# Causal attention with a full-array product ahead of each plain score, one DMA for each set of fixed rows, and another order of GpSimd's first steps

## The chip, the cores and the metric

The program runs on one NeuronCore of a Trainium2 chip. The metric is device time in microseconds (us), the median of three executions. Besides these one execution was taken with the hardware profiler; all rows of a trace shown here come from it.

## What is computed

A decoder of four layers on x of shape (8, 256, 128). Each layer adds an attention block and then a feed-forward block to x, each on a layer norm of x. The context has shape (8, 512, 128), and there are 16 heads of 8 dimensions. Layer 2 has a causal attention inside its feed-forward block, and this is the stage that the change touches most:

```python
def attention(x, wq, wk, wv, wo, bo):
    b, t, _ = x.shape
    q = (x @ wq).reshape(b, t, HEADS, HEAD_DIM)
    k = (x @ wk).reshape(b, t, HEADS, HEAD_DIM)
    v = (x @ wv).reshape(b, t, HEADS, HEAD_DIM)
    scores = jnp.einsum('bqhd,bkhd->bhqk', q, k)
    mask = jnp.arange(t)[:, None] < jnp.arange(t)[None, :]
    scores = jnp.where(mask, -jnp.inf, scores)
    attn = jax.nn.softmax(scores / np.sqrt(HEAD_DIM), axis=-1)
    ctx = jnp.einsum('bhqk,bkhd->bqhd', attn, v).reshape(b, t, EMB)
    return ctx @ wo + bo
```

The other attentions (layers 0 to 3, called A0 to A3) go over the 512 positions of the context, A2 with a mask.

## The kernel before

The stages run in the order A0, F0, A1, F1, A2, AS, F2, A3, F3 (PHASES): A are attentions, F feed-forward blocks, AS is the causal attention with 256 keys. Every engine has its own program, written out by hand, and they meet at semaphores. An attention stage has one body per batch (8), a body four groups `g` of four heads, and a group four steps `k`. A body on TensorE (`body` in `attention`) issues at each step, in this order: two plain scores, then transposed scores, then products of probabilities and values, and in fixed places one product of the projections (`misc`: XT, Q, K, V, turns of the head sums AVT0 and AVT1, ONT, O).

Plain scores (`scores`, L1032 to L1043) serve only to find the largest score of each row. Q and K of a head lie on a strip of 32 partitions, four heads on the four strips, each with its eight dimensions in several parts and some fixed rows. A plain score is one product, 32 rows high, of 128 queries with the keys; in AS only with the keys that the queries see, so 128 columns for the first half of the queries and 256 for the second. VectorE takes the maximum (`maximum`), in AS after adding `caus_q`. The scores run two groups ahead: those of a batch's groups 0 and 1 are issued in the body before, and the first two groups of AS in the last body of A2. GpSimd splits the maxima, TensorE turns them into rows of Q, and the transposed scores (`scores_T`) come out with the maximum already subtracted. In AS steps 0 and 3 of a group each hold two units of transposed scores: a product of 256 columns, one of 128, and the mask, which is a full-array product of the identity `ident_b` with `caus_T` (L1062). ScalarE takes the exponential, and `values` multiplies by V (L1086).

The parts of Q and K go through DRAM: SyncE (SP) saves them as rows of a scratch tensor and loads them back as strips (`save_k`, `save_q`, `load_strips`). A strip has 32 rows. Rows 1 to 24 are the parts; row 0 and rows 25 to 31 are fixed (ones where the maxima and the keys' mask enter, zeros otherwise). They are made once: GpSimd lays a pattern into `fixed`, TensorE spreads it with a product with ones, VectorE copies it to `rows_q` and `rows_k`, and SP fills both buffers of the scratch (`fill_rows`), two DMAs for Q and two for K each time. Between the two fills SP issues the loads of F0's weights, of the rest of x and of the next context.

At the start GpSimd computes the power of -1/2 for the first quarter of x (`first_power(0)`), clears the value tile of batch 0 (`set_values(0)`), computes the other three powers, and only then normalises batch 0 (`normalise_batch`), which TensorE, ScalarE and GpSimd need for Q. VectorE takes the statistics of all of x, waits for the four powers and then quantises the weights of F0 (`quantise_weights`) before it takes the first maximum.

Of the kernel before, what the change touches and what calls it, by code (L numbers as in the profile page):

```python
# [36 lines left out]
B, S, D, SK = 8, 256, 128, 512  # L37
H, DH = 16, 8
NT = B * S // 128
QT = S // 128  # L40
HG = 4
STRIP = 32
K_ROWS = (1, 1 + 2 * DH, 1 + DH)
Q_ROWS = (1, 1 + DH, 1 + 2 * DH)
MAX_ROW = 1 + 3 * DH
MASK_ROWS = (0, MAX_ROW + 3)
NG = H // HG
TB = 4
NBLK = NT // TB
# [116 lines left out]
def build(nc, t, out):  # L166
    cnt = Counts()
    with ExitStack() as ctx:
# [6 lines left out]
        sig = {n: sem(n) for n in cnt.names}  # L175
# [52 lines left out]
        fixed = sb("fixed", [1, 2, 128])  # L228
# [180 lines left out]
        def _(sp):  # L409
# [11 lines left out]

            def fill_rows(p):

                for n, fill, w in (("q", rows_q, S), ("k", rows_k, SK)):
                    rest = scratch[n][p].rearrange("(h r) w -> r h w", h=H)
                    for r0, r1 in ((0, 1), (MAX_ROW, STRIP)):
                        sp.dma_start(rest[r0:r1], fill[r0:r1, :].rearrange("r (o w) -> r o w", o=1).to_broadcast([r1 - r0, H, w]))\
                          .then_inc(strips_filled[p], 16)

            def load_rest():  # L430

# [126 lines left out]
            for ph in PHASES:  # L558
                if ph not in ATT:
                    continue  # L560
                if ph != "AS":

                    if ph != "A0":
                        wait(sp, "v_ready", cnt.start("v_ready", ph))
                        first_contexts(ph)
                    if ph in ("A1", "A2"):

                        wait(sp, "o_ready", cnt.start("o_ready", ph))
                        a = {"A1": "A2", "A2": "AS"}[ph]
                        for i, w in enumerate("qkvo"):  # L570
                            sp.dma_start(w_att[a][:, i, :], t[f"{a}_{w}"]).then_inc(watt_in[a], 16)
                    if ph == "A0":
                        for p in range(2):
                            sp.wait_ge(strips_filled[p], 16 * 4)
                    if ph == "A3":
                        wait(sp, "max_done", cnt.start("max_done", ph))
                        save_mask(Batch(0))
                    wait(sp, "st_ready", cnt.start("st_ready", ph))
                    save_k(ph, Batch(0))
                    save_q(ph, Batch(0))  # L580
                    load_strips(ph, Batch(0))
                    next_context(ph, Batch(2))
                    if ph == "A3":
                        save_mask(Batch(1))
                    save_k(ph, Batch(1))
                    save_q(ph, Batch(1))
                    load_strips(ph, Batch(1))

                def body(bt, first, last):
                    nph, nbt = following(ph, bt, 2)  # L590
                    cph, cbt = following(ph, bt, 3)
                    if nph:
                        if nph == "A3":
                            save_mask(nbt)
                        if nph != "AS":
                            save_k(nph, nbt)
                        if cph and cph != "AS":
                            next_context(cph, cbt)
                        save_q(nph, nbt)
                        if nph == "AS":  # L600
                            save_k(nph, nbt)
                        wait(sp, "st_ready", cnt.at("st_ready", ph, bt, cnt.per[ph]["st_ready"] - 1))
                        load_strips(nph, nbt)
                    if ph in ("A1", "AS", "A3") and bt.b < 4:
                        load_ffn({"A1": "F1", "AS": "F2", "A3": "F3"}[ph], bt.b)

                batches(body)
                if ph == "A0":
                    load_rest()
# [8 lines left out]
        def _(pool):  # L618
# [3 lines left out]
            link(pool.memset(fixed[:, :, :], 0.0))  # L622
            link(pool.memset(ones_row[:, :], 1.0))
            for r in MASK_ROWS:
                pool.memset(fixed[:, 0, r:r + STRIP * (HG - 1) + 1:STRIP], 1.0)
            link(pool.memset(fixed[:, 1, :].rearrange("p (j r) -> p j r", j=HG)[:, :, MAX_ROW:MAX_ROW + 3], 1.0))
            pool.memset(w_att["A3"][:, 0:3, :], 0.0).then_inc(rows_made, 1)
            link(pool.memset(ident[:, :], 0.0))
            link(pool.affine_select(out=ident[:, :], in_=ident[:, :], compare_op=ALU.not_equal, fill=1.0, base=0, pattern=[[-1, 128]], channel_multiplier=1))
# [96 lines left out]
            def attention(ph):  # L726
                b0, b1 = Batch(0), Batch(1)
                if ph != "AS":
# [2 lines left out]
                    normalise_batch(ph, b0)  # L731
                    split_k(ph, b0)
                    split_q(ph, b0)
                    normalise_batch(ph, b1)
                    if ph == "A0":
                        set_values(1)
                    if ph == "A3":
                        prepare_masks(b1)
# [82 lines left out]
                pool.memset(vaug[p][:, :, :, DH:DH + 1], 1.0).then_inc(vaug_set, 1)  # L821

            first_power(0)
            set_values(0)
            for blk in range(1, NBLK):
                first_power(blk)
            for ph in PHASES:
                if ph in ATT:
                    attention(ph)
# [193 lines left out]
        def _(pe):  # L1023
# [8 lines left out]
            def scores(ph, bt, g, i):  # L1032
# [5 lines left out]
                if ph == "AS":  # L1038
                    nk = 128 * (q + 1)
                wait(pe, "max_done", cnt.at("max_done", ph, bt, 8 * g + i) - BACK[i])  # L1040
                dst = ps_s[TURN[i]][:, 0:nk]
                pe.matmul(dst, qst[p][strip, g, q * 128:(q + 1) * 128], kst[p][strip, g, 0:nk],  # L1042
                          start=True, stop=True).then_inc(sig["s_ready"], 1)  # L1043

            def scores_T(ph, bt, g, n, c):

# [761 lines left out]
```

## Time and profile before

| | us |
|---|---|
| median of three executions (2041.43 to 2043.42) | 2042.76 |
| the profiled execution | 2041.18 |
| its span, first to last instruction | 2039.4 |
| TensorE busy | 1857.1 (91%) |
| VectorE busy | 1151.3 (56%) |
| ScalarE busy | 1096.2 (54%) |
| GpSimd busy | 590.7 (29%) |
| mean granted clock of TensorE | 0.896 |

The page names the engines PE (TensorE), PEld (its weight loads), DVE (VectorE), ACT (ScalarE), POOL (GpSimd) and SPq (SP's queue). PEclk is the clock that was granted to TensorE as a share of 2.4 GHz, in tenths in the 40 slices of the span (9 is 0.9 or more). A row of the timeline has its start, its length, engine, line, operation, what it writes and reads, the rows and columns of the array that it uses, and its shape; "x4" are four instructions merged. A matmul's length contains its way through the array, so matmuls overlap, and the distance of starts tells what each one costs.

### The profile page before, as it was taken

Reading aid. Unit: us, or ns where it says so; the run is one execution under the profiler, and the core shown is the slowest. Engines: PE = TensorE matmul, PEld = TensorE weight load, DVE = VectorE, ACT = ScalarE, POOL = GpSimd, SP = SyncE. Lnnn points to the kernel's source line nnn. Section 1 sums busy time; section 2 is a strip of 40 time slices with the busy share of each in tenths; the row PEclk is TensorE's granted clock in tenths of the full one; section 3 lists DMA queues with packets and bytes.
Section 4 is the critical chain, followed back from the end, with each engine's and each line's share of the span. In section 5 each row is a group of like instructions: output and inputs, shape, how many; then the busy total and the mean of one; then the engine's idle time right before and its main releaser. Section 6 shows DMA issues by size and latency. Waiting matters only on the chain.

```text
span 2039.4 us, 38938 instructions
## 1 busy us (share of the span) xinstructions
PE 1857.1 (91%) x14476; PEld 1195.3 (59%) x14476; DVE 1151.3 (56%) x3394; ACT 1096.2 (54%) x2172; POOL 590.7 (29%) x1171
## 2 busy tenths in 40 slices
PE   3999965899979999899999999997997999989997
PEld 1455534455559988634444555556885455569997
DVE  4788845688842233267777533334664788834342
ACT  0788840588854444256666533333331788854443
POOL 4344312233221222123333422212333444212221
PEclk9999987799989999889999855557997899989999
DMA  4433200445300000132322322100002454100000
GB/s 121 130 120 120 72 16 25 130 150 170 97 7 1 1 1 1 59 114 81 115 69 68 99 82 64 55 25 1 1 1 69 140 160 148 57 1 6 6 6 6
DMA packets 114882, 132.38 MB, mean 65 GB/s; under 512 B 14962, under 2 KB 78728, under 8 KB 114696
## 3 DMA queue, kind: packets, MB, share of 16 engines
q1 hardware_dynamic: 114696, 129.90, 21.1%
q8 instruction: 117, 1.92, 0.4%
q14 instruction: 69, 0.57, 0.1%
HBM read 83.45 MB, written 46.40 MB: 64 GB/s over the span
## 4 chain that ended last, share of the span: by engine, by line
PE 77%; DVE 8%; issue 7%; ACT 4%; POOL 1%; DMA 1%; SPq 0%; POOLq 0%; DVEq 0%
PE ps_av L1086 13%; PE ps_s L1311 13%; PE ps_s L1042 13%; PE ps_t L1289 9%; PE ps_t L1058 5%; DVE mx L1443 4%; PE ps_s L1289 3%; PE ps_t L1071 3%; PE ps_m L1142 2%; PE ps_m L1094 2%; PE ps_m L1128 2%; ACT prob L851 2%; PE ps_m L1134 2%; PE ps_t L1062 2%; PE ps_m L1121 2%
## 5 line engine op out<-in xcount | busy, mean ns | idle before, releaser
L851 ACT ACTIVATE prob<-ps_t 128x512 f32<-128x512 f32 (+1 forms) x1152 | 628.9, 583 | 229.5 <-PE ps_t L1058 145.6
L1443 DVE TENSOR_REDUCE mx<-ps_s 128x1 f32<-128x512 f32 x768 | 491.2, 683 | 117.5 <-PE ps_s L1042 110.3
L1042 PE MATMUL ps_s<-kst,qst 32*128 32x512 f32 (+2 forms) x1280 | 380.8, 514 | 42.2 <-DVE mx L1443 26.7
L1086 PE MATMUL ps_av<-prob,vaug 128*32 128x256 f32 (+1 forms) x4608 | 379.3, 405 | 3.2 <-ACT avs L892 3.2
L1058 PE MATMUL ps_t<-qmx,kst 32*128 32x256 f32 (+1 forms) x2304 | 339.4, 347 | 0.1
L1042 PEld LDWEIGHTS ps_s<-kst,qst 32*128 32x128 f32 x1280 | 159.3, 204 | 274.6 <-issue 151.1
L1311 PEld LDWEIGHTS ps_s<-w_ffn,prob 128*128 128x128 f32 x2688 | 314.1, 192 | 8.3
L1311 PE MATMUL ps_s<-w_ffn,prob 128*128 128x128 f32 x2688 | 318.4, 275 | 0.0
L991 ACT ACTIVATE prob<-ps_t,b1c 128x512 f32<-128x512 f32 x204 | 125.3, 685 | 240.1 <-PE ps_t L1289 240.1
L1677 DVE SCALAR_TENSOR_TENSOR avs<-ps_s,comb,avs 128x128 f32<-128x128 f32 x336 | 94.6, 344 | 260.4 <-PE ps_s L1311 260.4
L788 POOL TENSOR_TENSOR kst<-w_ffn,kst 128x512 fp32r<-128x512 f32 x100 | 127.1, 1273 | 370.5 <-ACT kst L976 370.5
L1058 PEld LDWEIGHTS ps_t<-qmx,kst 32*128 32x128 f32 x2304 | 211.6, 197 | 21.5 <-issue 19.1
L1446 DVE CUSTOM_DVE_ANT_0 junk<-ps_s,mask_q 128x512 bf16<-128x512 f32 x256 | 167.7, 687 | 72.2 <-PE ps_s L1042 72.2
L692 POOL CAST mpart<-mx 128x8 bf16<-128x8 f32 x160 | 34.8, 218 | 587.4 <-DVE mx L1443 317.4
L1289 PE MATMUL ps_t<-k_hi,kst 128*128 128x512 f32 x600 | 184.7, 415 | 6.2 <-ACT xfT L953 2.4
L1086 PEld LDWEIGHTS ps_av<-prob,vaug 128*32 128x32 f32 x4608 | 94.6, 111 | 112.9 <-issue 44.4
L1446 DVE CUSTOM_DVE_ANT_0 junk<-ps_s,caus_q 128x128 bf16<-128x128 f32 (+1 forms) x256 | 82.6, 354 | 127.8 <-PE ps_s L1042 126.5
L1289 PEld LDWEIGHTS ps_t<-k_hi,kst 128*128 128x128 f32 x600 | 107.7, 193 | 28.1 <-DVE prob L1662 3.6
L647 POOL TENSOR_TENSOR rstd<-veps,neg_half 128x2 f32<-128x2 f32 (+1 forms) x60 | 48.4, 807 | 259.5 <-DVE means L1387 259.5
L896 ACT ACTIVATE qmx<-ps_m 128x256 fp32r<-128x256 f32 x160 | 61.8, 387 | 97.8 <-PE ps_m L1096 97.7
L1071 PE MATMUL ps_t<-mask_T,ident_b 128*128 128x512 bf16 x256 | 82.1, 388 | 5.3 <-ACT prob L851 3.6
L1289 PE MATMUL ps_t<-k_lo,kst 128*128 128x512 f32 x300 | 85.4, 393 | 0.0
(209 smaller groups left out, 2202.1 us busy)
## 6 DMA issues: line engine op xcount, KB each, us to landing
kst<-k_parts SPq DMA_DIRECT2D x128, 256.0 KB, 3.5
qst<-q_parts SPq DMA_DIRECT2D x160, 128.0 KB, 3.8
k_parts<-k_hi SPq DMA_DIRECT2D x64, 256.0 KB, 3.0
q_parts<-q_hi SPq DMA_DIRECT2D x80, 128.0 KB, 2.4
ctxT<-in_ctxT SPq DMA_DIRECT2D x32, 256.0 KB, 2.7
k_parts<-k_lo SPq DMA_DIRECT2D x32, 256.0 KB, 3.2
q_parts<-q_lo SPq DMA_DIRECT2D x40, 128.0 KB, 2.4
w_ffn<-in_F_w SPq DMA_DIRECT2D x18, 256.0 KB, 6.6
```

The source lines that it names most:

```text
L788: pool.tensor_tensor(halves(wl), first_weights(ph, e), halves(wh.bitcast(F32)), ALU.subtract).then_inc(sig["wl_done"], 1)
L851: nc.scalar.activation(row[:, S * kt:S * kt + w], ps_t[TURN[unit(ph, g, n) % 8]][:, 0:w], ACT.Exp).then_inc(sig["exp_done"], 1)
L991: nc.scalar.activation(h[:, c, :], src, ACT.Gelu, bias=b1c[:, 4 * e + c:4 * e + c + 1]).then_inc(sig["h_done"], 1)
L1042: pe.matmul(dst, qst[p][strip, g, q * 128:(q + 1) * 128], kst[p][strip, g, 0:nk], start=True, stop=True).then_inc(sig["s_ready"], 1)
L1058: mm = pe.matmul(dst, kst[p][strip, g, kt * 128:(kt + 1) * 128], qmx[strip, g % 2, seen(ph, kt):], start=mask in (None, "keys") or mask == ...
L1071: pe.matmul(ps_t[TURN[turn]][:, :].rearrange("p (c s) -> p c s", c=2), ident_b[:, :], mask_T[:, 2 * kp:2 * kp + 2, :], start=True, stop=False)
L1086: mm = pe.matmul(ps_av[32 * j:32 * j + 32, q0:S], vaug[p][:, kt, HG * g + j, :], prob[:, buf, j, S * kt:S * (kt + 1) - q0], start=(kt == 0 ...
L1289: mm = pe.matmul(ps_h[c][:, :], w[:, 128 * c:128 * (c + 1)], x[:, :], start=(n == 0), stop=(n == 2))
L1311: mm = pe.matmul(dst, h[:, c, 128 * q:128 * (q + 1)], w2c, start=(c == 0 and not bias), stop=(c == nc_h - 1))
L1443: dve.tensor_reduce(mx[:, buf, i:i + 1], src, AX.X, ALU.max, negate=True).then_inc(sig["max_done"], 1)
L1446: dve.tensor_tensor_reduce(junk[:, TURN[i], 0:nk], src, m, -1.0, 3.0e38, ALU.add, ALU.min, mx[:, buf, i:i + 1])\
L1677: ins = dve.scalar_tensor_tensor(out=acc[:, q, :], in0=src, scalar=comb[:, q, n:n + 1], in1=acc[:, q, :], op0=ALU.mult, op1=ALU.add)
```

## The change

In `scores`, each plain score of AS gets a product ahead of it into the same bank: `ident_b` times the columns 128 to 255 of the first block of `caus_T`, which are all zeros, over all 128 rows; the score then adds to it (`start=False`). That makes 256 products more, half of them of 128 columns and half of 256. The fixed rows move to the front of each strip (rows 0 to 7), so one DMA fills them for Q and one for K, from 128 partitions of `rows_q` and `rows_k` in place of eight. On GpSimd `set_values(0)` moves behind the split of batch 0's Q, and the other three first powers behind batch 1's normalisation.

```diff
@@ -40,9 +40,10 @@
 QT = S // 128
 HG = 4
 STRIP = 32
-K_ROWS = (1, 1 + 2 * DH, 1 + DH)
-Q_ROWS = (1, 1 + DH, 1 + 2 * DH)
-MAX_ROW = 1 + 3 * DH
+FIXED = 8
+K_ROWS = (FIXED, FIXED + 2 * DH, FIXED + DH)
+Q_ROWS = (FIXED, FIXED + DH, FIXED + 2 * DH)
+MAX_ROW = 1
 MASK_ROWS = (0, MAX_ROW + 3)
 NG = H // HG
 TB = 4
@@ -421,11 +422,8 @@
 
             def fill_rows(p):
 
-                for n, fill, w in (("q", rows_q, S), ("k", rows_k, SK)):
-                    rest = scratch[n][p].rearrange("(h r) w -> r h w", h=H)
-                    for r0, r1 in ((0, 1), (MAX_ROW, STRIP)):
-                        sp.dma_start(rest[r0:r1], fill[r0:r1, :].rearrange("r (o w) -> r o w", o=1).to_broadcast([r1 - r0, H, w]))\
-                          .then_inc(strips_filled[p], 16)
+                for n, fill in (("q", rows_q), ("k", rows_k)):
+                    sp.dma_start(scratch[n][p].rearrange("(h r) w -> h r w", h=H)[:, 0:FIXED, :], fill).then_inc(strips_filled[p], 16)
 
             def load_rest():
 
@@ -571,7 +569,7 @@
                             sp.dma_start(w_att[a][:, i, :], t[f"{a}_{w}"]).then_inc(watt_in[a], 16)
                     if ph == "A0":
                         for p in range(2):
-                            sp.wait_ge(strips_filled[p], 16 * 4)
+                            sp.wait_ge(strips_filled[p], 16 * 2)
                     if ph == "A3":
                         wait(sp, "max_done", cnt.start("max_done", ph))
                         save_mask(Batch(0))
@@ -622,8 +620,8 @@
             link(pool.memset(fixed[:, :, :], 0.0))
             link(pool.memset(ones_row[:, :], 1.0))
             for r in MASK_ROWS:
-                pool.memset(fixed[:, 0, r:r + STRIP * (HG - 1) + 1:STRIP], 1.0)
-            link(pool.memset(fixed[:, 1, :].rearrange("p (j r) -> p j r", j=HG)[:, :, MAX_ROW:MAX_ROW + 3], 1.0))
+                pool.memset(fixed[:, 0, r:r + FIXED * (H - 1) + 1:FIXED], 1.0)
+            link(pool.memset(fixed[:, 1, :].rearrange("p (h r) -> p h r", h=H)[:, :, MAX_ROW:MAX_ROW + 3], 1.0))
             pool.memset(w_att["A3"][:, 0:3, :], 0.0).then_inc(rows_made, 1)
             link(pool.memset(ident[:, :], 0.0))
             link(pool.affine_select(out=ident[:, :], in_=ident[:, :], compare_op=ALU.not_equal, fill=1.0, base=0, pattern=[[-1, 128]], channel_multiplier=1))
@@ -731,8 +729,12 @@
                     normalise_batch(ph, b0)
                     split_k(ph, b0)
                     split_q(ph, b0)
+                    if ph == "A0":
+                        set_values(0)
                     normalise_batch(ph, b1)
                     if ph == "A0":
+                        for blk in range(1, NBLK):
+                            first_power(blk)
                         set_values(1)
                     if ph == "A3":
                         prepare_masks(b1)
@@ -821,9 +823,6 @@
                 pool.memset(vaug[p][:, :, :, DH:DH + 1], 1.0).then_inc(vaug_set, 1)
 
             first_power(0)
-            set_values(0)
-            for blk in range(1, NBLK):
-                first_power(blk)
             for ph in PHASES:
                 if ph in ATT:
                     attention(ph)
@@ -1039,8 +1038,11 @@
                     nk = 128 * (q + 1)
                 wait(pe, "max_done", cnt.at("max_done", ph, bt, 8 * g + i) - BACK[i])
                 dst = ps_s[TURN[i]][:, 0:nk]
+                if ph == "AS":
+                    pe.matmul(dst.rearrange("p (c s) -> p c s", s=128), ident_b[:, :], caus_T[:, 0:1, 128:S].to_broadcast([128, q + 1, 128]),
+                              start=True, stop=False)
                 pe.matmul(dst, qst[p][strip, g, q * 128:(q + 1) * 128], kst[p][strip, g, 0:nk],
-                          start=True, stop=True).then_inc(sig["s_ready"], 1)
+                          start=ph != "AS", stop=True).then_inc(sig["s_ready"], 1)
 
             def scores_T(ph, bt, g, n, c):
```

TensorE, a stretch of a body of AS behind the first products with V of a group: two steps without transposed scores, the turn of the maxima between them (`L1094`, `L1096`; after the change `L1096`, `L1098`). Before:

```order
L1042 MATMUL ps_s<-kst,qst 128x128 x2
L1094 MATMUL ps_m<-qst,ident_r 128x256
L1096 MATMUL ps_m<-ident_b,mpart 128x128 x2
L1042 MATMUL ps_s<-kst,qst 128x256 x2
L1121 MATMUL ps_m<-xnT,w_A 128x256
L1086 MATMUL ps_av<-prob,vaug 32x128 x4
```

After, the same place:

```order
L1042 MATMUL ps_s<-caus_T,ident_b 128x128
L1044 MATMUL ps_s<-kst,qst 128x128
L1042 MATMUL ps_s<-caus_T,ident_b 128x128
L1044 MATMUL ps_s<-kst,qst 128x128
L1096 MATMUL ps_m<-qst,ident_r 128x256
L1098 MATMUL ps_m<-ident_b,mpart 128x128 x2
L1042 MATMUL ps_s<-caus_T,ident_b 128x256
L1044 MATMUL ps_s<-kst,qst 128x256
L1042 MATMUL ps_s<-caus_T,ident_b 128x256
L1044 MATMUL ps_s<-kst,qst 128x256
L1123 MATMUL ps_m<-xnT,w_A 128x256
L1088 MATMUL ps_av<-prob,vaug 32x128 x4
```

Each plain score now stands behind a product of 128 rows. Of the two pairs the first follows products with V, the second a product of 128 rows and 128 columns (`L1098`), as before.

TensorE at a step that also has transposed scores (`L1060`), after the change, behind the product of K (`L1130`):

```order
L1130 MATMUL ps_m<-xnT,w_A 128x256
L1042 MATMUL ps_s<-caus_T,ident_b 128x128
L1044 MATMUL ps_s<-kst,qst 128x128
L1042 MATMUL ps_s<-caus_T,ident_b 128x128
L1044 MATMUL ps_s<-kst,qst 128x128
L1060 MATMUL ps_t<-qmx,kst 128x256 x2
L1060 MATMUL ps_t<-qmx,kst 128x128
L1064 MATMUL ps_t<-caus_T,ident_b 128x2x128
L1060 MATMUL ps_t<-qmx,kst 128x128
```

The pair follows a full product here too; the transposed scores follow the second score.

GpSimd at the start, from the first power on. Before:

```order
L815 TENSOR_TENSOR rstd<-veps,neg_half 128x4
L820 MEMSET vaug 128x2048
L821 MEMSET vaug 128x64
L815 TENSOR_TENSOR rstd<-veps,neg_half 128x4 x3
L707 TENSOR_SCALAR xn<-x_tok,means,rstd 128x128 x2
L673 CAST k_hi<-kf 128x512
L675 TENSOR_TENSOR k_lo<-kf,k_hi 128x512
L681 CAST q_hi<-qf 128x256
L683 TENSOR_TENSOR q_lo<-qf,q_hi 128x256
L707 TENSOR_SCALAR xn<-x_tok,means,rstd 128x128 x2
L820 MEMSET vaug 128x2048
```

After:

```order
L817 TENSOR_TENSOR rstd<-veps,neg_half 128x4
L705 TENSOR_SCALAR xn<-x_tok,means,rstd 128x128 x2
L671 CAST k_hi<-kf 128x512
L673 TENSOR_TENSOR k_lo<-kf,k_hi 128x512
L679 CAST q_hi<-qf 128x256
L681 TENSOR_TENSOR q_lo<-qf,q_hi 128x256
L822 MEMSET vaug 128x2048
L823 MEMSET vaug 128x64
L705 TENSOR_SCALAR xn<-x_tok,means,rstd 128x128 x2
L817 TENSOR_TENSOR rstd<-veps,neg_half 128x4 x3
L822 MEMSET vaug 128x2048
```

The power's rows (`L815`, now `L817`) for the other three quarters move from ahead of batch 0's normalisation to behind batch 1's.

## Rows read from the trace of the kernel before

**Rows 1.** The page: busy time of each engine, and the granted clock in 40 slices.

```profile
PE 1857.1 (91%) x14476; PEld 1195.3 (59%) x14476; DVE 1151.3 (56%) x3394; ACT 1096.2 (54%) x2172; POOL 590.7 (29%) x1171
...
PEclk9999987799989999889999855557997899989999
```

**Rows 2.** Busy time by stretches: A2, then four of AS.

```profile
core 0: us, PE busy (x) PEld busy (x) DVE busy (x) ACT busy (x) POOL busy (x), PEclk, DMA share, GB/s
1000.00:1034.00 34.00, 33.42 (x313) 15.06 (x314) 24.85 (x88) 23.29 (x49) 13.06 (x29) 1.00 0.30 90
1143.00:1160.00 17.00, 16.30 (x143) 9.66 (x139) 9.68 (x64) 9.89 (x24) 9.08 (x23) 1.00 0.20 54
1160.00:1183.00 23.00, 22.93 (x122) 13.00 (x120) 8.93 (x53) 8.40 (x19) 6.03 (x18) 0.50 0.35 106
1183.00:1353.00 170.00, 168.18 (x907) 92.25 (x910) 62.29 (x379) 63.62 (x146) 40.55 (x117) 0.50 0.23 67
1353.00:1389.00 36.00, 31.11 (x173) 16.95 (x169) 8.77 (x45) 10.94 (x26) 3.10 (x10) 0.50 0.00 0
```

**Rows 3.** Timeline of TensorE, AS: start, length, line, tiles, shape; turns and K's products.

```profile
1140.72 0.60 PE L1142 MATMUL ps_m<-ident,avs 128*128 128x128 f32 x4
...
1152.24 0.60 PE L1128 MATMUL ps_m<-xnT,w_A 128*128 128x256 f32 x2
...
1216.03 1.06 PE L1128 MATMUL ps_m<-xnT,w_A 128*128 128x256 f32 x2
...
1231.61 1.06 PE L1142 MATMUL ps_m<-ident,avs 128*128 128x128 f32 x4
...
1250.05 1.06 PE L1128 MATMUL ps_m<-xnT,w_A 128*128 128x256 f32 x2
```

**Rows 4.** Timeline of TensorE, AS at granted clock 0.50.

```profile
1223.04 0.39 PE L1062 MATMUL ps_t<-caus_T,ident_b 128*128 128x256 bf16 x1
1223.36 0.47 PE L1058 MATMUL ps_t<-qmx,kst 32*128 32x128 f32 x1
1223.77 0.39 PE L1062 MATMUL ps_t<-caus_T,ident_b 128*128 128x256 bf16 x1
...
1226.78 0.47 PE L1042 MATMUL ps_s<-kst,qst 32*128 32x128 f32 x2
1227.18 0.58 PE L1094 MATMUL ps_m<-qst,ident_r 128*128 128x256 f32 x1
...
1227.93 0.58 PE L1042 MATMUL ps_s<-kst,qst 32*128 32x256 f32 x2
1228.44 0.66 PE L1086 MATMUL ps_av<-prob,vaug 128*32 128x128 f32 x8
```

**Rows 5.** Timeline of TensorE, AS at granted clock 1.00.

```profile
1147.58 0.28 PE L1062 MATMUL ps_t<-caus_T,ident_b 128*128 128x256 bf16 x1
1147.79 0.32 PE L1058 MATMUL ps_t<-qmx,kst 32*128 32x128 f32 x1
1148.05 0.28 PE L1062 MATMUL ps_t<-caus_T,ident_b 128*128 128x256 bf16 x1
```

**Rows 6.** Timeline of all engines, the first 45 us.

```profile
8.39 1.04 POOL L815 TENSOR_TENSOR rstd<-veps,neg_half 128x4 f32<-128x4 f32 x1
...
18.86 2.57 SPq L427 DMA_DIRECT2D k_parts<-prob  x2
...
25.57 1.01 POOL L815 TENSOR_TENSOR rstd<-veps,neg_half 128x4 f32<-128x4 f32 x1 [0.45 <-DVE means L1387]
...
28.81 1.21 SPq L496 DMA_DIRECT2D k_parts<-k_hi  x2
...
36.55 0.69 DVE L1472 TENSOR_REDUCE aw<-ps_av 128x4 f32<-128x512 f32 x1 [11.06 <-PE ps_av L1176]
...
38.30 0.80 PE L1042 MATMUL ps_s<-kst,qst 32*128 32x512 f32 x3 [1.89 <-DMA qst<-q_parts]
...
43.81 1.28 DVE L1443 TENSOR_REDUCE mx<-ps_s 128x1 f32<-128x512 f32 x2
```

## Prediction

> **What bounds the kernel now.** I read the page first: TensorE is busy for 91% of the span, and the row of granted clocks shows one long stretch of fives, slices 23 to 27, in a kernel that otherwise runs near full clock [rows 1]. Then the busy time by stretches [rows 2]. In A2, the masked attention, TensorE is busy for 33.4 of 34 us at clock 1.00. In the causal stage AS it is as busy (168.2 of 170 us), and the clock stands at 0.50 (1.2 of 2.4 GHz). It fell at about 1160, in the second batch's body of AS, after a stretch that was 96% busy, and did not come back before the stage's end. ScalarE, VectorE and GpSimd are busy for 64, 62 and 41 of those 170 us, so TensorE alone sets the pace of AS, and what an added product costs there is what it takes on TensorE.
>
> How long a body (one batch) takes at either level: from K's product to K's product is 34.0 us at 0.50; the stretch from the second turn of the head sums to K's product is 18.44 us at 0.50 and 11.52 at 1.00 [rows 3]. The ratio 0.625 makes a body 21.3 us at full clock, 12.7 less. That is the prize the full-array product could win; what matters is what it costs and whether it wins it.
>
> Now a pair of scores goes strip, strip, and its two products start together (x2 on one row, 0.40 us to the next product). With the change it goes full, strip, full, strip. Added are two full streams, one strip stream that ran beside the other, two exchanges to strip and one to full: at half clock 3 x 0.107 + 2 x 0.11 + 0.30 = 0.84 us for a pair of 128 columns and 3 x 0.213 + 0.52 = 1.16 for one of 256; at full clock 0.16 + 0.40 = 0.56 and 0.32 + 0.40 = 0.72. Where a full product stands ahead of the pair (two of a group's four pairs: those of steps 0 and 2), the exchange it pays today goes: minus 0.11. A group has two pairs of each width: 2 x 0.84 + 2 x 1.16 - 0.22 = 3.8 us at half clock, 2 x 0.56 + 2 x 0.72 - 0.22 = 2.35 at full. A batch (four groups): 15.1 and 9.4 us. Both ends of this price: if every exchange hid behind a running product, only 16 x 128 + 16 x 256 = 6144 columns would be left, 5.1 us a batch at half clock, 2.6 at full; nothing makes it cheaper, since TensorE has no idle time there. The upper end is 16.0 at half clock, every pair paying its whole exchange. I take 15.1: the measured exchanges are between the same two shapes with the same identity as weights.
>
> The Trainium skill says the same in "TensorE: Matmul & The Clock Gate", Part 3: small products run side by side when they lie in different row groups, and a weight load overlaps a running product only if its row group differs; a full-array load shares a row group with everything. The trace agrees (strip pairs start together, the mask product does not).
>
> **Does the clock hold?** At full clock the body would grow from 21.3 to 30.7 us; of the 9.4 added, 2.6 stream columns through the whole array and 6.8 are exchanges or strips that no longer run side by side. In A2, which keeps 1.00, a step adds two masks of 512 columns, nearly all streaming [rows 2]. So AS gains work for the array but spreads its own over 44% more time, and it fell before after 1.25 bodies at full clock. I forecast that it falls again, about in the middle of the first body, and stays down: at half clock the body is 34.0 + 15.1 = 49 us, and of the 15.1 only 5.1 stream columns through the whole array, so the stage grows longer faster than it grows denser.
>
> **Sum for AS.** The scores run two groups ahead, so the 32 groups lie thus: two in A2's last batch and two in AS's first body at full clock, 4 x 2.35 = 9.4 us; 28 at half clock, 28 x 3.8 = 106. The clock falls 0.75 body earlier in the work: 0.75 x 12.7 = 9.5. Together +125 us. Everything else of AS stays (F2 starts at half clock today too), and VectorE, ScalarE and the DMAs have more time, so they hide as before.
>
> **The start.** GpSimd today waits with batch 0's normalisation until the last power at 25.57, which needs all of x; K, Q and V of batch 0, and behind them VectorE's weight quantisation, begin late (36.55), and the first maximum comes at 43.81 [rows 6]. With the change xn follows the first power, which ends at 9.4. From the last power's end, 26.6, to the quantisation takes 10.0 us today, so what lies between is done near 20. VectorE still needs all four powers: 26.6, or some 2.4 us sooner, since one DMA for each fill takes SP about 0.6 (as each k_hi save: 1.21 for two) and not 1.3 (2.57 for two), and the x load lies behind one set of four. The quantisation takes 43.81 - 36.55 = 7.3: VectorE is free at 31.5 to 33.9. The scores need batch 0's strips: from first save to first score is 9.5 us today (28.81 to 38.30), some 8.5 when q waits with k; the save waits for the second fill. Its issue ends at 21.4 today, 16.7 then; landing 3 us later gives scores at 28; landing as late as today gives 37. So the first maximum comes at 31.5 to 37.5: 6 to 12 us won. I take 11, since 128 partitions are read in place of eight. No later step waits for a fixed time, so it stays. GpSimd's clearing of the value tile (two memsets, about 2 us) now stands ahead of ScalarE's V copy; the maximum's start covers it.
>
> **Total.** 2041.2 (profiled execution) + 125 - 11 = 2155; the median of the runs is 1.6 higher and I round to **2155 us**.
>
> **The rivals.**
> A, *the clock holds* although the exchanges cost what I say. For it: the products are of the full array, A2 and F2 hold 1.00 with such. Against: AS fell in a 96% busy stretch. Seven bodies of 30.7 make 215 in place of 222 (from 1131, a body of 21.3 before K's last product at full clock, to 1353), A2's end +4.7, the last 36 us [rows 2] at 0.625 plus two groups 27.2 (-8.8): -11, start -11: **2019**. It decides if the granted clock is 1.00 through AS.
> B, *the exchanges hide and the clock holds*: bodies 21.3 + 2.6 = 23.9, seven 167 (-55), last stretch -12, A2's end +1.3, start -11: **1964**. Against it: the exchange rows above.
> The Trainium skill speaks for B in the same page, Part 2: weights for the background buffer may be loaded ahead of products in flight, and Part 1 has the clock follow a busy engine. By these the change would win; the first is not what the mask product's rows show, and by the second AS should not have fallen at 96% busy.
> C, *the exchanges hide but the clock falls*: 28 x 1.28 + 4 x 0.64 + 9.5 - 11 = +37: **2078**.
> D, *the clock falls late*: each body that stays at full clock saves 49.1 - 30.7 = 18.4; three more make **2100**.
> E, *start alone counts*, the two effects in AS cancelling: near 2041.
>
> **Chances.** Forecast 0.68, D 0.08, C 0.06: slower by over 0.2% 0.82 (0.2%, 4 us, is about what a measurement of this kernel can tell from none). A 0.08, B 0.07: faster 0.15. E 0.03. The forecast's own range is 2125 to 2178 (price per group 3.4 to 4.0, fall anywhere from A2's end to the second body, start 6 to 12). The range takes in C and D: 2072 to 2178, and leaves out A, B and E.
>
> **What would show it.** Right: the clock row at fives from the first batch of AS on, K's product to K's product 49 us, full-strip-full starts 0.3 to 0.4 apart, an AS busy near 100%; the first maximum near 33. Wrong: tens through AS (A or B; the body's length, 31 or 24, tells which), or a body of 39 us at half clock (C).

## The result, and the profile after

The changed kernel takes 2152.46 us (median of three, 2150.2 to 2155.99) against 2042.76: ratio 1.054, 95% interval 1.0516 to 1.0565. Its profiled execution took 2150.20 us, with a span of 2148.4, 109.0 us over that of before. The page, as in [rows 1]:

```profile
PE 1976.9 (92%) x14691; PEld 1261.6 (59%) x14732; DVE 1164.3 (54%) x3394; ACT 1097.5 (51%) x2172; POOL 592.9 (28%) x1171
...
PEclk9999976999899998999995555555999699999999
```

TensorE is busy for 119.8 us more; the row of the clock has seven fives in place of the four of [rows 1]. The busy time by stretches, as in [rows 2]: A2, the first 11 us of AS, then AS at half clock:

```profile
core 0: us, PE busy (x) PEld busy (x) DVE busy (x) ACT busy (x) POOL busy (x), PEclk, DMA share, GB/s
989.00:1023.00 34.00, 32.95 (x308) 15.04 (x316) 24.85 (x87) 23.27 (x49) 13.30 (x30) 1.00 0.30 90
1124.00:1135.00 11.00, 11.00 (x86) 5.88 (x85) 4.41 (x29) 4.39 (x10) 3.59 (x9) 1.00 0.51 148
1136.00:1166.00 30.00, 30.00 (x135) 16.68 (x135) 9.68 (x51) 7.05 (x16) 6.72 (x15) 0.50 0.01 3
1167.00:1359.00 192.00, 192.00 (x847) 103.98 (x845) 56.02 (x306) 50.52 (x116) 34.78 (x95) 0.50 0.19 55
```

The clock falls at 1135.4, in the first body of AS, while TensorE is busy without a gap. The timeline of K's products, as in [rows 3]:

```profile
1088.19 0.70 PE L1130 MATMUL ps_m<-xnT,w_A 128*128 128x256 f32 x2
1123.29 0.70 PE L1130 MATMUL ps_m<-xnT,w_A 128*128 128x256 f32 x2
1166.53 1.06 PE L1130 MATMUL ps_m<-xnT,w_A 128*128 128x256 f32 x2
1214.73 1.06 PE L1130 MATMUL ps_m<-xnT,w_A 128*128 128x256 f32 x2
1262.93 1.06 PE L1130 MATMUL ps_m<-xnT,w_A 128*128 128x256 f32 x2
```

From the third on they stand 48.2 us apart; before it was 34.0. The stretch that ends A2 and issues the first two groups of AS, 1088.19 to 1123.29 (called A2's last body below), went from 30.7 to 35.1. The pairs of scores at 0.50, to be read beside [rows 4]:

```profile
1219.12 0.29 PE L1042 MATMUL ps_s<-caus_T,ident_b 128*128 128x128 bf16 x1
1219.34 0.47 PE L1044 MATMUL ps_s<-kst,qst 32*128 32x128 f32 x1
1219.75 0.29 PE L1042 MATMUL ps_s<-caus_T,ident_b 128*128 128x128 bf16 x1
1219.96 0.47 PE L1044 MATMUL ps_s<-kst,qst 32*128 32x128 f32 x1
1220.37 0.39 PE L1042 MATMUL ps_s<-caus_T,ident_b 128*128 128x256 bf16 x1
1220.69 0.58 PE L1044 MATMUL ps_s<-kst,qst 32*128 32x256 f32 x1
1221.20 0.39 PE L1042 MATMUL ps_s<-caus_T,ident_b 128*128 128x256 bf16 x1
```

and at 1.00, beside [rows 5]:

```profile
1126.02 0.23 PE L1042 MATMUL ps_s<-caus_T,ident_b 128*128 128x128 bf16 x1
1126.18 0.32 PE L1044 MATMUL ps_s<-kst,qst 32*128 32x128 f32 x1
1126.43 0.23 PE L1042 MATMUL ps_s<-caus_T,ident_b 128*128 128x128 bf16 x1
```

Full to strip and strip to full take 0.22 and 0.41 us at half clock for 128 columns (0.32 and 0.51 for 256), 0.16 and 0.25 at full clock. Less the columns these are exchanges of 0.11 and 0.30, and of 0.10 and 0.20. The rows of the weight loads (PEld) give these sizes a name:

```profile
1219.34 0.28 PEld L1044 LDWEIGHTS ps_s<-kst,qst 32*128 32x128 f32 x1
1219.74 0.10 PEld L1042 LDWEIGHTS ps_s<-caus_T,ident_b 128*128 128x128 bf16 x1
```

A score's weights load in 0.28 us, the zero product's in 0.10 (0.18 and 0.10 at full clock). From one start to the next passes, within 0.02 us, the first product's own load and its columns: 0.10 + 0.11 and 0.28 + 0.11. So I read an exchange as a weight load that no longer runs beside the product ahead of it; no run here changes the weights' type to test that.

The start, timeline of all engines, as in [rows 6]:

```profile
9.61 1.59 POOL L705 TENSOR_SCALAR xn<-x_tok,means,rstd 128x128 f32<-128x128 f32 x2
9.64 0.43 SPq L553 DMA_DIRECT2D x_tok<-in_x  x1
...
12.07 0.60 SPq L426 DMA_DIRECT2D k_parts<-prob  x1
...
18.29 1.16 SPq L494 DMA_DIRECT2D k_parts<-k_hi  x2
19.12 3.07 POOL L817 TENSOR_TENSOR rstd<-veps,neg_half 128x4 f32<-128x4 f32 x3
...
22.29 0.69 DVE L1474 TENSOR_REDUCE aw<-ps_av 128x4 f32<-128x512 f32 x1 [1.18 <-POOL rstd L817]
...
27.10 0.80 PE L1044 MATMUL ps_s<-kst,qst 32*128 32x512 f32 x3 [6.35 <-DMA qst<-q_parts]
...
30.33 1.28 DVE L1445 TENSOR_REDUCE mx<-ps_s 128x1 f32<-128x512 f32 x2
```

The same VectorE instructions in both traces show where the difference arises. At the first maximum the changed kernel is 13.5 us ahead, from the middle of A0 on 12.5, from F0's end to A2 11.2; where A3 begins it is 110.9 behind, and at the end 109.0. So the start gives 11.2, AS with F2 costs 122.1, and A3 and F3 give 1.9 back.

### The profile page after: what moved, and what is told of

It is laid out like the page before. It is cut to its first block, busy times and chain, and to the rows that moved or that the text cites. A ratio compares the mean times of both kernels' runs of the same rounds, so it can differ in the third digit from the quotient of the medians.

```text
span 2148.4 us, 39405 instructions
## 1 busy us (share of the span) xinstructions
PE 1976.9 (92%) x14691; PEld 1261.6 (59%) x14732; DVE 1164.3 (54%) x3394; ACT 1097.5 (51%) x2172; POOL 592.9 (28%) x1171
## 4 chain that ended last, share of the span: by engine, by line
PE 79%; DVE 8%; issue 7%; ACT 4%; POOL 1%; DMA 1%; SPq 0%; POOLq 0%; DVEq 0%
PE ps_s L1044 15%; PE ps_av L1088 12%; PE ps_s L1313 12%; PE ps_t L1291 8%; PE ps_t L1060 5%; DVE mx L1445 4%; PE ps_s L1291 3%; PE ps_s L1042 3%; PE ps_t L1073 3%; PE ps_m L1096 2%; PE ps_m L1144 2%; PE ps_m L1130 2%; ACT prob L850 2%; PE ps_t L1064 2%; PE ps_m L1136 2%
## 5 line engine op out<-in xcount | busy, mean ns | idle before, releaser
L1044 PE MATMUL ps_s<-kst,qst 32*128 32x512 f32 (+2 forms) x1280 | 447.4, 519 | 43.0 <-DVE mx L1445 25.1
L1044 PEld LDWEIGHTS ps_s<-kst,qst 32*128 32x128 f32 x1280 | 195.3, 207 | 283.4 <-issue 155.7
L1060 PE MATMUL ps_t<-qmx,kst 32*128 32x256 f32 (+1 forms) x2304 | 341.7, 349 | 0.0
L1060 PEld LDWEIGHTS ps_t<-qmx,kst 32*128 32x128 f32 x2304 | 213.6, 198 | 21.9 <-issue 20.9
L1448 DVE CUSTOM_DVE_ANT_0 junk<-ps_s,caus_q 128x128 bf16<-128x128 f32 (+1 forms) x256 | 91.5, 357 | 226.6 <-PE ps_s L1044 223.3
L1042 PE MATMUL ps_s<-caus_T,ident_b 128*128 128x128 bf16 (+1 forms) x256 | 86.6, 338 | 0.0
```

What stands on the lines that cost most here:

```text
L1042: pe.matmul(dst.rearrange("p (c s) -> p c s", s=128), ident_b[:, :], caus_T[:, 0:1, 128:S].to_broadcast([128, q + 1, 128]), start=True, st ...
L1060: mm = pe.matmul(dst, kst[p][strip, g, kt * 128:(kt + 1) * 128], qmx[strip, g % 2, seen(ph, kt):], start=mask in (None, "keys") or mask == ...
L1448: dve.tensor_tensor_reduce(junk[:, TURN[i], 0:nk], src, m, -1.0, 3.0e38, ALU.add, ALU.min, mx[:, buf, i:i + 1])\
```

## Experiments

Every ratio is to runs of the kernel before on the same chip. That kernel itself spread there: in the first set 25 runs lie at 2040 to 2046 us (8) and at 2051 to 2058 (17), median 2052.87. Profiled runs of four kernels whose AS is the same code give a likely reason. Counted from the K product in AS's first body, the clock fell after 30 us in the kernel before and in start_only (at 1160 and 1150), and after 15 us in fill_only and gpsimd_only (at 1148 and 1141). Each us of full-clock work done at half clock costs 0.6 more, so these 15 us are worth 9. No execution of the upper group of the kernel before was profiled.

**The parts alone.** start_only is the changed kernel without the added product (four lines of `scores` as before), product_only the kernel before with only that; gpsimd_only has only the moved calls of `set_values(0)` and `first_power`, fill_only only the rows' new places and the single DMAs:

```diff
 start_only, against the changed kernel
-                if ph == "AS":
-                    pe.matmul(dst.rearrange("p (c s) -> p c s", s=128), ident_b[:, :], caus_T[:, 0:1, 128:S].to_broadcast([128, q + 1, 128]),
-                              start=True, stop=False)
...
-                          start=ph != "AS", stop=True).then_inc(sig["s_ready"], 1)
+                          start=True, stop=True).then_inc(sig["s_ready"], 1)
```

> The change without its zero product: one DMA for each fill and the new order of GpSimd. Theory (the two parts of the change add up, the start is worth 11 us behind the first layers): 2031 us (2029 to 2033), first maximum at 30 us as in the changed kernel, clock row as before the change. Rival (part of the gain seen in the changed kernel, 13.5 us at the first maximum and 11.2 at the end of A2, is only there because of how the stages then meet the clock): over 2035 or under 2027.

Measured 2039.37 us, ratio 0.9953 (0.9934 to 0.9972); first maximum at 30.26. The total missed the expected 2031 and lies where the rival had it, but the kernel before had a median of 2052.87 in this set. The profiled run, 2028.1 at mean clock 0.897, is the only one of eleven below 2038; the others had 0.888 to 0.890. In its trace the start leaves 10.6 us at the end of A2; the total alone does not show the gain's size.

> Only the zero product ahead of each plain score of AS; the start as before the change. Theory (the loss is all in AS, worth 122 us there): 2164 us (2160 to 2168), K's product to K's product 48.2 us at granted clock 0.50. Rival (AS starts at another phase of whatever lowers the clock, and keeps full clock for another part of it): under 2150.

Measured 2152.96 us, ratio 1.0521 (1.0469 to 1.0573): under the expected 2160 to 2168 and not under the rival's 2150. In its profiled run the clock held until 1175, so its first body of AS ran wholly at full clock: K's products at 1137.6 and 1168.5, 30.9 us; those at half clock stand 48.2 apart. The rival's mechanism is there (another 37 us of AS at full clock, against 12 in the changed kernel). It explains why the changed kernel, with the better start, is not faster than this one: it comes to K's product in AS's first body 14.3 us sooner (1123.29 for 1137.61), and takes 91.4 us for the two bodies from there where product_only takes 75.0.

> Only the new order of GpSimd at the start; the fixed rows are filled by two DMAs each as before. Theory (the normalisation comes early, but VectorE's statistics of the rest of x wait for a load that SP issues behind four fill DMAs, and the three powers still come at about 25 us): first maximum between 36 and 40 us where it was 43.8, so 2035 to 2040 us. Rival (order alone is the whole gain): 2031 us. Rival (nothing without the earlier load): 2042 us.

> Only the fixed rows in front of each strip and one DMA for each fill; GpSimd in its old order, normalisation behind all four powers. Theory (x's rest lands 4.4 us earlier, so the powers end 4.4 us earlier and with them all that follows): first maximum near 39.5 us, 2038 us (2036 to 2040). Rival (SP's fill was hidden anyway): 2042 us. Rival (it is most of the gain): 2031 us.

Measured 2046.85 (ratio 0.9993, 0.9972 to 1.0014) and 2048.2 us (0.9981, 0.9963 to 0.9999): neither reached its expected total, and neither can be told from no change by it with confidence. The first maxima of the profiled runs are near what was expected: 43.81 before, 37.16 with the order alone, 38.27 with the fill alone, 30.26 with both. So they gain 6.6 and 5.5 us, and 13.5 together. What is left of it hangs on the clock. In fill_only the first rise came at 79.4 (before 67.9), and the 5.5 us were gone by 100; gpsimd_only was 3.9 ahead at the end of A2 and lost 9.1 in AS to its earlier fall. With the order alone GpSimd has K's parts by 14 us, but SP saves them only at 27.60, behind the second fill; with the fill alone they are made at 22.56 and saved at 23.27.

**What the price consists of.** Three kernels add as many zero columns, 6144 a batch, as the change. paired_order keeps the change but issues both full products of a step first:

```diff
+                                    if ahead[0] == "AS":
+                                        for n in (2 * k, 2 * k + 1):
+                                            opening(*ahead, n)
                                     for n in (2 * k, 2 * k + 1):
                                         if ahead[0]:
                                             scores(*ahead, n)
```

> The changed kernel with the two zero products of a step first and its two scores behind them, in place of full, strip, full, strip: the same 6144 columns a batch, fewer exchanges. Theory (two thirds of the price are exchanges): at half clock a group costs 0.21 (128 columns, full product ahead) + 0.62 (128) + 0.43 (256, full ahead) + 0.84 (256) = 2.1 us over the kernel before in place of 3.55, a body 42.4 us in place of 48.2, 30 groups 43 us less: 2109 us (2095 to 2120). Rival (the price hangs on columns and the number of products, not on their order): 2152. Rival (the clock now holds, since the array streams more of the time): under 2000.

Measured 1985.08 us (three executions 1968 to 1990, the fourth, left out of the ratio, 2025), ratio 0.9649 (0.9601 to 0.9698). The second rival came true: the clock stayed at 1.00 nearly to the stage's end (a short fall at 1160, then 1300). Page and timeline of paired_order; K's products are 24.2 us apart:

```profile
PEclk9999977699989999969999999959996899989999
```

```profile
1201.08 0.60 PE L1136 MATMUL ps_m<-xnT,w_A 128*128 128x256 f32 x2
...
1209.05 0.28 PE L1037 MATMUL ps_s<-caus_T,ident_b 128*128 128x128 bf16 x2
1209.26 0.33 PE L1050 MATMUL ps_s<-kst,qst 32*128 32x128 f32 x2
1209.52 0.38 PE L1102 MATMUL ps_m<-qst,ident_r 128*128 128x256 f32 x1
...
1225.25 0.60 PE L1136 MATMUL ps_m<-xnT,w_A 128*128 128x256 f32 x2
```

Two full products, one exchange, two strips side by side: the theory of the exchanges holds too. A pair is added at 0.21 us here, not 0.56. Where it ran at half clock (from 1300) full products and strips start 0.32 apart for 128 columns, two streams and one exchange.

strip_rows makes the added product 32 rows high:

```diff
-                    pe.matmul(dst.rearrange("p (c s) -> p c s", s=128), ident_b[:, :], caus_T[:, 0:1, 128:S].to_broadcast([128, q + 1, 128]),
+                    pe.matmul(dst.rearrange("p (c s) -> p c s", s=128), ident_b[strip, :], caus_T[strip, 0:1, 128:S].to_broadcast([STRIP, q + 1, 128]),
```

> The changed kernel with its zero product 32 rows high, on the strip of the score that it opens, in place of 128 rows: as many products and columns, no change of shape. Theory: only the stream of one of the two is exposed, 2 x 0.107 + 2 x 0.213 = 0.64 us a group at half clock, a body 36.6 us; with the start's gain 2048 to 2070 us. Rival (a further product into a bank costs its issue and its weights whatever its height): body 48 us, 2150. Its zeros are added all the same; nothing of the computation is left out.

Measured 2020.89 us, ratio 0.9877 (0.9848 to 0.9905): faster than expected. At half clock a body takes 34.3 us, so 32 products more cost 0.3 us, not 2.6. Timeline at 0.50:

```profile
1243.36 0.29 PE L1042 MATMUL ps_s<-caus_T,ident_b 32*128 32x128 bf16 x2
1243.40 0.46 PE L1044 MATMUL ps_s<-kst,qst 32*128 32x128 f32 x2
1243.79 0.58 PE L1096 MATMUL ps_m<-qst,ident_r 128*128 128x256 f32 x1
```

The four still occupy 0.43 us before the full product, where two occupied 0.40 [rows 4]. So neither the number of products nor columns that stream beside other strips are what the change pays for; the height of 128 rows is. The ledger of the 14.2 us that the change adds to a body: 5.1 for the full columns, 2.6 for scores that ran beside another, 6.5 for exchanges, less than the two thirds that I expected for paired_order. The clock fell at 1174, after two bodies of 22.3 and 21.7 us.

**Full columns where the shape does not change.** dense_mask has the new start, no product ahead of the scores, and the same 6144 columns behind the masks:

```diff
                     mm = pe.matmul(bank[:, :].rearrange("p (c s) -> p c s", c=2)[:, :, 0:128], ident_b[:, :],
-                                   caus_T[:, 0:1, 0:128].to_broadcast([128, 2, 128]), start=False, stop=True)
+                                   caus_T[:, 0:1, 0:128].to_broadcast([128, 2, 128]), start=False, stop=False)
+                    mm = pe.matmul(bank[:, 0:384].rearrange("p (c s) -> p c s", s=128), ident_b[:, :],
+                                   caus_T[:, 0:1, 128:S].to_broadcast([128, 3, 128]), start=False, stop=True)
```

> The kernel before with the new start and no product ahead of the scores; in its place a zero product of 384 columns, full array, right behind each of the 16 mask products of a body of AS, where the shape does not change. Theory A (full columns without exchanges keep the clock up): granted clock 1.00 through AS, a body 21.3 + 16 x 0.16 = 23.9 us, and F2 starts at full clock: 1950 to 1960 us. Theory B (AS falls all the same): a body 34.0 + 16 x 0.32 = 39.1 us at half clock, 2070 to 2085 us.

Measured 1969.19 us (1967.6 to 1984.4), ratio 0.9648 (0.9599 to 0.9696): the clock and the body of theory A, the time 9 us over its range. The clock fell at 1309, where AS ends, and F2 did not start at full clock. Timeline and stretches of AS:

```profile
1191.06 0.59 PE L1129 MATMUL ps_m<-xnT,w_A 128*128 128x256 f32 x2
1214.93 0.59 PE L1129 MATMUL ps_m<-xnT,w_A 128*128 128x256 f32 x2
```

```profile
1167.00:1287.00 120.00, 116.49 (x985) 64.75 (x985) 61.38 (x381) 63.64 (x146) 41.43 (x121) 1.00 0.33 96
```

A body is 23.9 us. TensorE is busy for 97% of the time at 1.00, less than the changed kernel's 100% at 0.50. dense_mask_turn adds 256 columns in each turn (`maxima_T`):

> As dense_mask, with one more zero product of 256 columns inside the turn of the maxima of each group of AS, between two full-array products. Theory A (clock holds): 0.43 us a body more, 1953 to 1963 us. If the clock holds here and falls in dense_mask, the stretch without masks in the middle of a group decides. Theory B (falls): 0.85 us a body more, 2076 to 2092 us.

Measured 1986.11 us, ratio 0.9706 (0.9678 to 0.9734), over the 1953 to 1963 of theory A. The body is 24.3 as expected, but in the profiled run the clock fell in the last body, at 1290, and F2 began at half clock. dense_small has only 128 zero columns behind each mask:

> As dense_mask with 128 zero columns behind each mask in place of 384. Theory (it is a matter of dose; the first two bodies of AS sit just under what the clock wants): the clock falls within AS's first three bodies, a body then 34.0 + 16 x 0.11 = 35.7 us, 2030 to 2055 us. Rival (any full product more holds it): a body 22.2 us at clock 1.00, 1950 to 1957 us.

Measured 1992.16 us, ratio 0.9747 (0.972 to 0.977). Neither the theory nor the rival: it fell, but at 1237, in the sixth body; at full clock a body took 22.4. Behind the masks it looks like a matter of dose, and a third of the dose already holds it for five bodies; but dense_mask_turn, with more columns than dense_mask, fell 19 us sooner. dense_turn puts the 6144 columns in other places (128 behind each mask, four products of 256 ahead of each turn):

> As dense_mask, with the same 6144 zero columns a body elsewhere: 128 behind each mask, 4 x 256 at the head of each turn of the maxima. Theory (what counts is the stretch of each group that has no masks, where dense_mask was least dense): clock 1.00 through all of AS, a body 23.9 us, 1960 to 1970 us with less spread than paired_order's 1968 to 2025. Rival (the turn is on a chain that VectorE's maxima and the transposed scores wait for, so 0.43 us ahead of it shows): a body over 25 us, 1980 us.

Measured 1978.94 us (1962 to 1985), ratio 0.9659 (0.9622 to 0.9696), body 23.7. The turn costs nothing extra, but the time is over the 1960 to 1970 of the theory and the spread did not go: the profiled run fell at 1287. dense_last is dense_mask with four products of 512 columns in the last body:

```diff
+                                    if ph == "AS" and not ahead[0] and k in (1, 2):
+                                        wait(pe, "max_done", cnt.at("max_done", ph, bt, 8 * NG - 1))
+                                        pe.matmul(ps_s[k][:, :].rearrange("p (c s) -> p c s", s=128), ident_b[:, :],
+                                                  caus_T[:, 0:1, 128:S].to_broadcast([128, 4, 128]), start=True, stop=True)
```

> dense_mask, and in groups 2 and 3 of AS's last body, where no further scores are issued and where three of the kernels lost the clock (dense_mask_turn at 1290, dense_turn at 1287, paired_order at 1300), one zero product of 512 columns in each of the two steps without masks: 4 in all, 0.9 us at full clock. Theory: a body 23.9 us at clock 1.00 as in dense_mask, the clock falls only at the stage's end, no run over 1975, median 1960 to 1970 us. Rival (the fall there does not hang on what streams in those steps): the same spread as dense_turn, 1962 to 1985, median near 1980.

Measured 1981.44 us (1966 to 1987), ratio 0.9666 (0.9633 to 0.9698): a miss, the spread is that of dense_turn. The profiled execution (1968.78) kept the clock to 1312, so no trace shows where the slower ones lost it; filling those steps did not narrow the spread.

**The price with the clock held.** price_at_full is the changed kernel with the further products of dense_mask_turn.

> The changed kernel, its zero product ahead of each plain score in place, with the further zero products of dense_mask_turn (384 columns behind each mask, 256 in each turn) so that the clock has a chance to hold. Theory (the exchanges cost 2.2 us a group at full clock, as between the K products 1088.19 and 1123.29 of the changed kernel, and the clock follows how densely columns stream, not the number of changes of shape): granted clock 1.00 through AS, a body 24.3 + 8.8 = 33.1 us, 1970 + 7.5 bodies x 8.8 = 2036 us, 2054 if it falls in the last body as in dense_mask_turn. Rival (the exchanges themselves bring the clock down): a body at half clock, 48.2 + 16 x 0.32 + 0.85 = 54 us, 2190 us. Rival (at full clock the exchanges hide, as rival B had it): a body 27 us, 1990 us.

Measured 2047.53 us, ratio 1.0023 (1.0009 to 1.0037), between the two times of the theory. Timeline and stretches:

```profile
1188.43 0.60 PE L1135 MATMUL ps_m<-xnT,w_A 128*128 128x256 f32 x2
1220.83 0.59 PE L1135 MATMUL ps_m<-xnT,w_A 128*128 128x256 f32 x2
```

```profile
1188.00:1318.00 130.00, 130.00 (x931) 75.08 (x932) 54.13 (x300) 51.20 (x117) 34.84 (x98) 1.00 0.25 72
```

All the exchanges of the change are there and the clock stays at 1.00 until 1356: the exchanges do not lower it by themselves. A body is 32.4 us against 24.3 in dense_mask_turn, 8.1 for four groups. This kernel also pays for the further columns: 1.5 us a body against product_only's 30.9, 2.2 in dense_mask_turn against the 22.1 of the kernel before. Without them, and with the clock held as here, its profiled 2046.5 would be 2029 to 2035, an estimate from these rows. So with the clock held the change would have gained about what its start is worth.

## Why the prediction was right, point by point

**Sum.** Forecast 2155, measured 2152.5; the profiled execution 2150.2. The 2.9 us by which AS was set too high (125 for 122.1) and the 1.9 that A3 and F3 gave explain nearly all of the 4.8 between them. With the 1.6 for the median my sum gives 2156.8, not the 2155 that I rounded to. The four fives of the clock row are also not the five slices that I read.

**The price.** Forecast a group 3.8 us at half clock, 2.35 at full. Measured 14.2 a body, 3.55 a group; at full clock A2's last body gives 4.4 for two groups, 2.2 each, product_only's first body 8.8 over 22.1, and price_at_full 8.1. The body at full clock before the change I took as 21.3 from a ratio; the first one takes 22.1. Each exchange came as read from [rows 4, 5]. The steps of one body tell where 0.9 us of the 15.1 stayed away: pairs with a full product ahead added 0.72 us (128 columns) and 1.04 (256), those behind products with V 0.84 and 1.16, all as worked out. For instance the transposed scores start 1.00 us behind K's product before (1216.03 to 1217.03) and 1.72 now (1214.73 to 1216.45), and 0.59 behind products with V before (1221.83 to 1222.42) and 1.75 now (1222.78 to 1224.53). But three pairs a body more than the eight I counted have a full product of the projections ahead (ONT, AVT0, V): 0.3 us. And the kernel before waited once a body, in the stretch 1183 to 1353 (the waits of TensorE: us in total, times, longest):

```profile
PE ps_s L1042 <- DVE mx L1446: 1.4, 5, 0.3
```

In the changed kernel TensorE waits for nothing in 1167 to 1359: the slower pairs took 0.3 us a body of that. My "TensorE has no idle time there" was wrong by it. Of the last 0.3 half lies at the pair behind ONT, which added only 0.57; the rest stays open.

**The clock.** Forecast: it falls about the middle of the first body and stays down. It fell 12.1 us into a body that takes 31 at full clock, at 1135.4, and stayed down to the stage's end and into F2. The ledger: A2's last body +4.4 (forecast 4.7), the first two bodies of AS 43.2 + 48.2 in place of 22.1 + 29.8, so +39.5 (36.9), bodies 2 to 6 5 x 14.2 = 71.0 (75.7), and by the same price 7.1 (7.6) for the last body's two groups: 122.0. The fall was 0.98 body earlier in the work than before, not 0.75.

The reason I gave, that the stage grows longer faster than it grows denser, is supported from two sides. The same columns with fewer exchanges (paired_order) or with none added (dense_mask) held the clock nearly or wholly to the stage's end, and the same exchanges with more full columns held it in price_at_full. What the gate counts no trace shows. That the fall came sooner is not shown to be the change's doing: the unchanged AS fell after 15 us in two profiles and after 30 in two, the changed one after 12, and after 37 in product_only. Its place in the first body was in part luck, and so are the 12 us (0.98 x 12.7) of the 122 that hang on it; the other 110 are the price.

The Trainium skill ("TensorE: Matmul & The Clock Gate", Part 1) ties the clock to how busy TensorE has been and puts a fall down to idle time. These traces disagree: 100% busy at 0.50 in the changed kernel, 97% busy at 1.00 in dense_mask. By Part 3 of the same page of the Trainium skill a weight load overlaps a product in flight only where its row group differs. The pairs of scores agree (x2 rows of strips start together, and from a strip to a full product pass 0.41 us). strip_rows does not: there a score's load starts with the product ahead of it on the same strip, and both are in flight from 1243.40 on.

**The start.** Forecast -11 in the end and the first maximum near 33; measured 30.33 and 11.2 left in A2. The step that was off: I let x's load gain 2.4 us by shorter fills. It was issued 5.9 us earlier (15.54 to 9.64), because the load of F0's weights behind the fills issued in 0.42 us where it had taken 4.24 (0.42 in fill_only, 4.16 in gpsimd_only); the statistics began 4.4 us earlier. So the powers ended at 22.2, and VectorE was free at 30.1. The first score came at 27.1, near my early end of 28, by two errors: the second fills were issued by 12.7, not 16.7, but the save behind them began 5.6 us later, not 3. Of the 13.5 us 2.3 were lost, by these rows to the clock: its first rise came 26.5 us behind the first maximum (before 24.1), and in F0 the stretch at half clock behind A0 was 20.5 us long (17.1). So "no later step waits for a fixed time, so it stays" was wrong in that much, and the sum was right by two errors of 2 us against each other. It was also luck in part: of the ten profiled kernels with this start eight came to AS 10.6 to 12.5 us sooner than the kernel before, but paired_order 5.2 and strip_rows 6.9, where the first rise came at 71 in place of 54 to 61.

**The rivals.** A (the clock holds, 2019) was put at 0.08. It failed in its premise, and by the estimate from price_at_full its 2019 was also 10 to 16 us too low. B and C needed hidden exchanges, which no kernel shows where shapes alternate. D needed a fall some three bodies later; the alternating products kept full clock for 37 us at most without further columns. The median is inside the forecast's own range, 2125 to 2178.

## What to carry to other kernels

A zero product that is to feed the array belongs beside products of its own shape. Ahead of 32-row products it breaks up their running side by side and costs 0.36 to 0.58 us a time at half clock, nearly half of it (6.5 of 14.2 us a batch) without a column moving; behind the masks the same columns cost some 2 us a batch (23.9 for 22.1) and held the clock. That was worth 3.5% together with the new start, which alone gave 0.5%. Where a stage is busy and still at half clock, look at what shapes stream in it, not at its busy share; and take as many profiles as it needs to see how far the fall wanders before reading a difference of 10 us as an effect of the code.

## What was unexpected

A 32-row product ahead of another on the same strip cost 0.3 us a batch in all (34.3 for 34.0 at half clock); it is covered on the way to the next full product. A load that SP issues behind four fills from eight partitions took 4.24 us to issue, 0.42 behind two from 128 partitions. Kernels of identical AS code lost the clock anywhere from 1141 to 1160, and the variants that mostly hold it vary by some 20 us (paired_order 1968 to 1990, with one at 2025; dense_turn 1962 to 1985); what decides the late falls stays open, since filling the last body's steps did not narrow the spread.
